# Turning node rows for the matrix multiplications: by VectorE squares and DMAs in place of TensorE transposes

## What is computed

```python
h = relu(layernorm(x));  x = x + layer1(layer0(h))
h = relu(layernorm(x));  x = x + layer2(h)
# a layer, for one graph:
u = h @ h.T / sqrt(384);  delta = softmax(u) * adjacency
attn = delta / (sum(delta, -1) + 1e-10)
ctx = upper(attn) @ (h @ wl.T + bl) + diag(attn) * (h @ ws.T + bs) + lower(attn) @ (h @ wr.T + br)
out = relu((ctx - mean(ctx)) / sqrt(var(ctx) + 1e-12) * g + beta)
```

## Time and profile before

| | |
|---|---|
| median of 3 runs | 1308.77 us (1308.66 to 1308.91) |
| profiled execution | 1309.04 us, of which the profile's span is 1307.3 us |
| TensorE (PE) busy | 1293.1 us, 99% |
| VectorE (DVE) busy | 978.3 us, 75% |
| ScalarE (ACT) busy | 854.4 us, 65% |
| GpSimd (POOL) busy | 339.5 us, 26% |
| mean granted TensorE clock | 0.994 of full speed |
| DMA engines busy | 12.9% of 16 engines, 41 GB/s |

### The profile page before, as it was taken

One profiled execution on the slowest core, in us unless ns is written; L12 is line 12 of the kernel. 1 busy time (PEld: TensorE's weight loads), 2 busy tenths in 40 slices (PEclk: granted clock), 3 DMA queues, 4 the chain that ended last, 5 costly groups with the idle time before them and its releaser, 6 DMA issues.

```text
span 1307.3 us, 28090 instructions
## 1 busy us (share of the span) xinstructions
PE 1293.1 (99%) x7820; PEld 1262.4 (97%) x7820; DVE 978.3 (75%) x3057; ACT 854.4 (65%) x2141; POOL 339.5 (26%) x438
## 2 busy tenths in 40 slices
PE   7999999999999999999999999999999999999997
PEld 5999999999999999999999999999999999999997
DVE  5777777777777677777777777778787878788776
ACT  5766666666667666666666666676666666666664
POOL 1323222222223321211111111243232332323231
PEclk8999999999999999999999999999999999999999
DMA  4101010101011110101001010130101010101111
GB/s 144 55 29 42 28 42 28 42 28 42 28 48 60 43 29 29 42 28 42 28 28 42 28 39 31 47 97 17 43 28 42 28 42 28 41 29 36 34 34 47
DMA packets 44932, 52.98 MB, mean 41 GB/s; under 512 B 3552, under 2 KB 44128, under 8 KB 44896
## 3 DMA queue, kind: packets, MB, share of 16 engines
q1 hardware_dynamic: 44896, 52.54, 12.9%
HBM read 39.94 MB, written 12.58 MB: 40 GB/s over the span
## 4 chain that ended last, share of the span: by engine, by line
PE 97%; issue 1%; DMA 1%; DVE 0%; ACT 0%; SPq 0%; POOL 0%; POOLq 0%; DVEq 0%
PE right_bank L395 23%; PE left_bank L395 23%; PE context_bank L395 23%; PE context_bank L438 16%; PE score_bank L367 5%; PE node_bank L355 5%; PE score_bank L375 1%; PE edge_bank L387 1%; DMA rows<-x 1%; ACT weight L562 0%; DVE context L744 0%; DVE in_stats L632 0%; POOL rstd L858 0%; DVE node_t L647 0%; POOLq L130 0%
## 5 line engine op out<-in xcount | busy, mean ns | idle before, releaser
L395 PE MATMUL right_bank<-weight,node_t 128*128 128x384 f32 x1728 | 368.4, 353 | 0.9 <-ACT source L491 0.9
L395 PE MATMUL left_bank<-weight,node_t 128*128 128x384 f32 x1728 | 366.6, 352 | 0.0
L395 PE MATMUL context_bank<-weight,node_t 128*128 128x384 f32 x1728 | 346.0, 343 | 0.0
L395 PEld LDWEIGHTS left_bank<-weight,node_t 128*128 128x128 f32 x1728 | 297.8, 189 | 10.6
L395 PEld LDWEIGHTS context_bank<-weight,node_t 128*128 128x128 f32 x1728 | 301.2, 188 | 3.1
L395 PEld LDWEIGHTS right_bank<-weight,node_t 128*128 128x128 f32 x1728 | 293.1, 189 | 11.2 <-issue 1.0
L438 PE MATMUL context_bank<-side_parts,attn_t 128*128 128x386 f32 x1152 | 241.1, 345 | 0.9 <-issue 0.8
L647 DVE SCALAR_TENSOR_TENSOR node_t<-node_bank,node_t 128x384 fp32r<-128x384 f32 x192 | 106.9, 557 | 155.8 <-ACT node_t L496 152.7
L438 PEld LDWEIGHTS context_bank<-side_parts,attn_t 128*128 128x128 f32 x1152 | 201.2, 190 | 1.4 <-issue 1.4
L858 POOL TENSOR_TENSOR rstd<-spread,scalars 128x2 f32<-128x2 f32 x96 | 90.2, 939 | 320.0 <-DVE spread L727 320.0
L550 ACT ACTIVATE context_bank<-context_bank,diag 128x386 f32<-128x386 f32 x192 | 105.1, 547 | 98.4 <-PE context_bank L395 98.4
(11 more groups left out here) (64 smaller groups left out, 1565.9 us busy)
## 6 DMA issues: line engine op xcount, KB each, us to landing
rows<-x SPq DMA_DIRECT2D x32, 384.0 KB, 3.2
residual_x<-x SPq DMA_DIRECT2D x32, 384.0 KB, 3.2
out<-rows SPq DMA_DIRECT2D x31, 384.0 KB, 2.6
adj_in<-adj SPq DMA_DIRECT2D x96, 64.0 KB, 2.1
piece<-weights SPq DMA_DIRECT2D x18, 192.0 KB, 2.6
rows<-weights SPq DMA_DIRECT2D x3, 576.0 KB, 9.3
vector_rows<-vectors SPq DMA_DIRECT2D x3, 576.0 KB, 5.7
vector_rows<-vectors SPq DMA_DIRECT2D x3, 384.0 KB, 6.1
```

The costliest lines, as they stand in the source:

```text
L395: mm = nc.tensor.matmul(bank[:, 0:D], node_t[:, s.parity, k, c, a], weight[:, s.phase % 2, w, c, b], start=False, stop=(c, a) == (CH - 1, ...
```

## The change

The transposes of `source` on TensorE and their two PSUM banks go. `source` becomes a view of a buffer `nodes`. ScalarE's `fill_source` now applies the relu too. VectorE's new `turn_nodes` turns all of it in one instruction, each 32 x 32 square within itself, into `turned`. SyncE's new `move_nodes` waits for that and then issues 16 DMAs, one for each pair of a source and a destination quarter of the partitions, each of 32 partitions by 192 numbers (24 KB), SBUF to SBUF, which put the squares in their places in `nodes` (the view `moved`). When all 16 have landed, ScalarE copies both tiles to `node_t` (high part) in one instruction, and VectorE makes the low part of both in one. `nodes` is single: the rows of a step are filled in only after those of the step before have been split.

The two free PSUM banks make `side_bank` double (one for each k), so `seed_side` waits for the tile before the last. Three orders change: ScalarE's body (both `fill_source` stand together behind `copy_cross`), VectorE's body (`input_shift` stands ahead of the left `split_side`, `turn_nodes(after)` behind the scores) and SyncE's (x is loaded one step earlier, and `move_nodes(after)` stands ahead of the store). The residual of phase 1 is loaded into `rows` in place of a buffer of its own. GpSimd's order stays. In the diff below the places where only names or counts follow suit are left out.

```diff
@@ -54,6 +54,9 @@
...
 PIECES = 3 * CH
+Q = 32
+QUARTERS = P // Q
+RUN = 2 * CH * Q
@@ -177,13 +180,15 @@
         first_raw = rows[:, TILES - PIECES:TILES]
-        side_bank = [bank("left_bank"), bank("right_bank")]
+        side_bank = [[bank("left_bank0"), bank("left_bank1")], [bank("right_bank0"), bank("right_bank1")]]
         context_bank = [bank("context_bank0"), bank("context_bank1")]
-        node_bank = [bank("node_bank0"), bank("node_bank1")]
...
         scores4 = score_bank[:, :].rearrange("p (k a j) -> p k a j", k=2, a=2)
-        node_3 = [b[:, 0:D].rearrange("p (c r) -> p c r", c=CH) for b in node_bank]
+        source = nodes[:, :].rearrange("p (k d) -> p k d", k=2)
+        source_blocks = nodes[:, :].rearrange("p (n q y) -> p q n y", q=QUARTERS, y=Q)
+        moved = nodes[:, :].rearrange("p (a e) -> p a e", a=QUARTERS)
+        moved_rows = nodes[:, :].rearrange("p (a n r) -> p n a r", a=QUARTERS, r=Q)
@@ -250,6 +256,10 @@
             return vector_rows[:, phase % 2, v * D:(v + 1) * D + extra]
+        def node_rows(s, part):
+            return node_t[:, s.parity, :, :, part].rearrange("p k c (a r) -> p (k c) a r", r=Q)
@@ -268,8 +278,9 @@
             def load_residual(s):
-                at_least(sp, post_done, s.tile(0))
-                sp.dma_start(residual_x[:, :, :], x_pairs[bass.ds(s.g, 1)].rearrange("g p k d -> p (g k) d")).then_inc(residual_in, 16)
+                at_least(sp, post_done, s.tile(0) - 2)
+                sp.dma_start(rows[:, bass.ds(2 * s.g, 2), :],
+                             x_pairs[bass.ds(s.g, 1)].rearrange("g p k d -> p (g k) d")).then_inc(residual_in[s.parity], 16)
@@ -302,10 +313,17 @@
...
                   .then_inc(out_written[s.parity], 16)
+            def move_nodes(s):
+                sp.wait_ge(nodes_turned, s.n + 1)
+                for a in range(QUARTERS):
+                    for q in range(QUARTERS):
+                        sp.dma_start(moved[q * Q:(q + 1) * Q, a], turned[a * Q:(a + 1) * Q, q]).then_inc(nodes_in, 16)
             def body(s):
-                prev, nxt, after = s.ahead(-1), s.ahead(1), s.ahead(2)
-                if after.exists() and after.phase == 0:
-                    load_x(after)
+                prev, nxt, after, third = s.ahead(-1), s.ahead(1), s.ahead(2), s.ahead(3)
+                if third.exists() and third.phase == 0:
+                    load_x(third)
@@ -315,6 +333,8 @@
...
                     load_norm_rows(s.phase + 1)
+                if after.exists():
+                    move_nodes(after)
@@ -328,11 +348,14 @@
...
             load_x(Step(0, 0, 1))
+            move_nodes(Step(0, 0, 0))
...
             load_first(SELF)
+            load_x(Step(0, 1, 0))
             load_norm_rows(0)
+            move_nodes(Step(0, 0, 1))
@@ -345,21 +368,10 @@
...
         def _(pe):
-            def nodes_ready(s, k):
-                pe.wait_ge(source_ready, s.tile(k) + 1)
-                at_least(pe, node_lo, s.tile(k) - 1)
-            def transpose_nodes(s, k, c):
-                mm = nc.tensor.transpose(node_bank[k][:, c * P:(c + 1) * P], source[:, k, c * P:(c + 1) * P], ident)
-                if c == CH - 1:
-                    mm.then_inc(node_moved, 1)
             def scores(s):
-                pe.wait_ge(node_hi, s.tile(2))
-                pe.wait_ge(node_lo, s.tile(2))
+                pe.wait_ge(node_hi, s.n + 1)
+                pe.wait_ge(node_lo, s.n + 1)
@@ -409,14 +419,12 @@
...
                         pe.wait_ge(piece_lo, (s.phase - 1) * PIECES + (w + 1) * CH)
-            def project_side(s, k, side, turned=None):
-                pe.wait_ge(node_hi, s.tile(k) + 1)
-                pe.wait_ge(node_lo, s.tile(k) + 1)
+            def project_side(s, k, side):
+                pe.wait_ge(node_hi, s.n + 1)
+                pe.wait_ge(node_lo, s.n + 1)
...
                 weights_split(s, k, side)
-                if turned is not None:
-                    nodes_ready(*turned)
-                project(s, k, side, side_bank[side], side_product[side], turned=turned)
+                project(s, k, side, side_bank[side][k], side_product[side])
@@ -483,17 +487,17 @@
...
             def fill_source(s, k):
-                at_least(act, node_moved, s.tile(k) - 1)
+                at_least(act, node_lo, s.n)
                 if s.phase == 1:
-                    nc.scalar.activation(source[:, k:k + 1], rows[:, s.slot(k)], ACT.Copy).then_inc(source_ready, 1)
+                    nc.scalar.activation(source[:, k:k + 1], rows[:, s.slot(k)], ACT.Relu).then_inc(source_ready, 1)
...
                     act.wait_ge(in_shift_done, s.normal + 1)
-                    nc.scalar.activation(source[:, k:k + 1], rows[:, s.slot(k)], ACT.Identity, bias=in_shift[:, k:k + 1],
+                    nc.scalar.activation(source[:, k:k + 1], rows[:, s.slot(k)], ACT.Relu, bias=in_shift[:, k:k + 1],
                                          scale=in_rstd[:, k:k + 1]).then_inc(source_ready, 1)
-            def split_nodes(s, k):
-                act.wait_ge(node_moved, s.tile(k) + 1)
-                nc.scalar.activation(node_t[:, s.parity, k, :, HI], node_3[k], ACT.Relu).then_inc(node_hi, 1)
+            def split_nodes(s):
+                act.wait_ge(nodes_in, 16 * QUARTERS * QUARTERS * (s.n + 1))
+                nc.scalar.activation(node_rows(s, HI), moved_rows, ACT.Copy).then_inc(node_hi, 1)
@@ -528,14 +532,14 @@
...
                 bias_rows_here(s, k)
-                at_least(act, side_lo[side], s.tile(k))
-                nc.scalar.activation(side_bank[side][:, 0:D], vector_row(s.phase, ROW_LEFT + side), ACT.Copy)\
+                at_least(act, side_lo[side], s.tile(k) - 1)
+                nc.scalar.activation(side_bank[side][k][:, 0:D], vector_row(s.phase, ROW_LEFT + side), ACT.Copy)\
...
                 at_least(act, context_product, s.tile(k))
-                nc.scalar.activation(side_parts[:, side, HI, 0:D], side_bank[side][:, 0:D], ACT.Copy).then_inc(side_hi[side], 1)
+                nc.scalar.activation(side_parts[:, side, HI, 0:D], side_bank[side][k][:, 0:D], ACT.Copy).then_inc(side_hi[side], 1)
@@ -565,26 +569,25 @@
...
                 if nxt.exists():
-                    split_nodes(nxt, 0)
+                    split_nodes(nxt)
...
                 seed_side(s, 1, RIGHT)
-                if nxt.exists():
-                    split_nodes(nxt, 1)
+                if len(pieces) > 0:
+                    split_piece(*pieces[0])
                 split_side(s, 0, LEFT)
+                seed_side(s, 1, LEFT)
...
                     split_edges(s)
-                seed_side(s, 1, LEFT)
...
                     copy_cross(nxt)
-                if len(pieces) > 0:
-                    split_piece(*pieces[0])
-                seed_self(s, 1)
...
                     fill_source(after, 0)
+                    fill_source(after, 1)
                 split_side(s, 1, RIGHT)
+                seed_self(s, 1)
@@ -592,12 +595,10 @@
...
                 if nxt.exists():
+                    seed_side(nxt, 0, LEFT)
+                scale_self(s, 1)
+                if nxt.exists():
                     seed_self(nxt, 0)
-                scale_self(s, 1)
-                if nxt.exists():
-                    seed_side(nxt, 0, LEFT)
-                if after.exists():
-                    fill_source(after, 1)
@@ -642,11 +642,15 @@
...
                                                ALU.mult, ALU.mult).then_inc(in_shift_done, 1)
-            def split_nodes(s, k):
-                dve.wait_ge(node_hi, s.tile(k) + 1)
-                nc.vector.scalar_tensor_tensor(node_t[:, s.parity, k, :, LO], node_3[k], 0.0,
-                                               node_t[:, s.parity, k, :, HI].bitcast(F32),
-                                               ALU.max, ALU.subtract).then_inc(node_lo, 1)
+            def turn_nodes(s):
+                dve.wait_ge(source_ready, s.tile(2))
+                at_least(dve, nodes_in, 16 * QUARTERS * QUARTERS * s.n)
+                nc.vector.transpose(turned[:, :, :], source_blocks).then_inc(nodes_turned, 1)
+            def split_nodes(s):
+                dve.wait_ge(node_hi, s.n + 1)
+                nc.vector.tensor_tensor(node_rows(s, LO), moved_rows, node_rows(s, HI).bitcast(F32), ALU.subtract).then_inc(node_lo, 1)
@@ -749,17 +753,20 @@
...
                 if s.phase == 1:
-                    dve.wait_ge(residual_in, 16 * (s.n + 1 - PAIRS))
-                other = residual_x[:, k:k + 1] if s.phase == 1 else rows[:, s.slot(k)]
-                nc.vector.scalar_tensor_tensor(rows[:, s.slot(k)], context[:, k:k + 1], 0.0, other, ALU.max, ALU.add).then_inc(post_done, 1)
+                    dve.wait_ge(residual_in[s.parity], 16 * (s.half + 1 - PAIRS // 2))
+                nc.vector.scalar_tensor_tensor(rows[:, s.slot(k)], context[:, k:k + 1], 0.0, rows[:, s.slot(k)], ALU.max, ALU.add).then_inc(post_done, 1)
...
                     input_stats(after, 0)
-                if nxt.exists():
```

(55 more changed lines are left out.)

26 lines of the change are left out of this document (10 added, 16 removed).

## The result

The changed kernel takes 1997.68 us (median of 4 runs, 1995.89 to 1997.97) against 1308.78 us before in the same runs: ratio 1.526, 95% interval 1.523 to 1.529. The direction was forecast; the size was not. 1747 us were predicted, and 1998 lies above the range.

The account below looks back on a forecast made before the run. A ring through five engines was to bound each step: engine work plus 8.65 us of DMAs, 18.0, 17.0 and 18.5 us in phases 0, 1, 2. Thirty-two of each are 1712 us, with start and tail 1747; range 1580 to 1850.

Parts of the forecast that it names:

- the term of the 16 DMAs: SP's queue, each step: fifteen distances of 0.43 us, 6.45 us; with beginning and landing 8.65 us.
- The landing: End of the moves: 2.1 us from a DMA's issue to its landing, taken from the 64 KB load.
- ring without DMAs: The engines' part of a step, from landing to first DMA issue: 9.3, 8.4 and 9.8 us by phase.
- the turn: VectorE's `turn_nodes`, 768 elements: 0.95 us, at the rate of element-wise operations, bounds 0.56 and 1.9.
- The ring: Five-engine loop from one landing of the 16 DMAs to the next; a step cannot be shorter: 18.0, 17.0, 18.5 us.
- the copies: After the landing, 768 elements each: ScalarE's copy to `node_t` 0.90 us, VectorE's `split_nodes` about 0.95 us.
- VectorE's wait for `in_rstd`: Ahead of `input_shift`, VectorE waits about 1.6 us for GpSimd in phases 0 and 2, not in phase 1.
- The clock: TensorE, idling 3 to 5 us a step, may run at half clock: costs little, or up to 96 us.
- TensorE's path: Scores, right projection and `turn_cross` end some 6 us behind the landing, against 7.8 for VectorE's path to `sum_scores`.
- Hidden moves: Rival: the ring stays hidden; faster below 0.13 us a distance, 1255 us where TensorE bounds; 7%.
- Cheap issues: Rival: SP's distances at the floor of 0.33 us, 1603 us; 15% for 1580 to 1650.
- Dear moves: Rival, with low clock: distances at 0.51 add 115 us, landing of 3.2 adds 106, slow turn 91; 16% for over 1840.

Follow-up runs that it names:

- e3: Changed kernel with its 16 moves replaced by 16 DMAs, four each of four forms (three within SBUF, one from device memory): 1932.0 us.
- e4: Changed kernel with its 16 moves replaced by eight DMAs of 128 partitions x 384 bytes, four within SBUF, four from device memory: 1464.4 us.
- e1: Changed kernel with 8 of the 16 moves of a step left out (destination quarters 2 and 3): 1481.2 us.
- e7: Changed kernel with the last 6 of 16 moves a step issued from ScalarE's queue, the first 10 from SyncE's: 1622.2 us.
- e8: Changed kernel with `nodes` double, rows filled, turned and moved three steps ahead, GpSimd and VectorE reordered, one weight piece buffer, all moves kept: 1337.6 us, ratio 1.021.
- e5: Changed kernel with GpSimd making the input's rstd ahead of the output's: 1944.3 us.
- e6: Changed kernel with 36 matmuls of unused result added on TensorE ahead of the scores, to keep it busy: 1970.8 us.
- e2: Changed kernel with 15 of the 16 moves of a step left out: 1276.4 us, ratio 0.976 against the kernel before.
- e11: Changed kernel with 12 DMAs replacing the 16 moves: four within SBUF, four SBUF to device memory, four device memory to SBUF: 1621.8 us.

## Why the prediction was wrong

**What failed: the term of the 16 DMAs.** "These are smaller (24 KB), so I take 0.43, with ends at 0.33 and 0.51." They stand 0.628 us apart, outside both ends and over the 0.5 us that the prediction itself named as a sign of being wrong: 15 x 0.198 x 96 = 285 us too little. Two things were wrong in that step. I took the highest of the three mixed distances of the earlier trace rows, 0.51, as a ceiling, where even plain loads in a row stand 0.50 apart in e3 and e4; and I let the size count in the small ones' favour, which e3 and e4 exclude. The SBUF to SBUF part, 0.1 on top, no row of before could show; the range should have been open upwards there. The landing went the other way, 1.8 us for 2.1, 29 us too much.

By phase, a step is the distance from the first of its 16 issues to the first of the next 16 (phase 0 from 310.03 to 330.04, phase 1 from 1018.19 to 1038.57 and 1059.02, phase 2 from 1515.56 to 1536.41):

```profile
1018.19 10.02 SPq L321 DMA_DIRECT2D nodes<-turned  x16
...
1038.57 10.01 SPq L321 DMA_DIRECT2D nodes<-turned  x16
...
1059.02 10.02 SPq L321 DMA_DIRECT2D nodes<-turned  x16
```

| step, us | predicted | measured |
|---|---|---|
| phase 0 | 18.0 | 20.0 |
| phase 1 | 17.0 | 20.4 |
| phase 2 | 18.5 | 20.85 |
| ring without DMAs, phase 0 | 9.3 | 8.7 |
| ring without DMAs, phase 1 | 8.4 | 9.1 |
| ring without DMAs, phase 2 | 9.8 | 9.6 |
| the turn (part of the ring), and 16 DMAs' issue and landing | 0.95 + 8.65 | 0.98 + 11.3 |

Thirty-two times the three differences are about 250 us, all that was missed. The engines' part of the ring came out right in the sum partly by luck: 0.6 and 0.2 us too much in phases 0 and 2, 0.7 too little in phase 1.

**What held.** The ring as the bound (e1, e7 and e8 shortened or opened it in three ways, and 516, 375 and, with e5's 53 in it, 660 us went), its parts on the engines within 0.7 us, the turn at 0.95 (0.98), the copies at 0.90 and 0.95 (0.84 and 0.96), VectorE's wait for `in_rstd` at 1.6 (1.51), TensorE busy 73% where 70 were said, and who waits for whom. ScalarE's wait for the moves was 7.8 us a step where some 5 were said, and not the longest of all: VectorE's behind it has 765.3 us in all, ScalarE's 751.4.

**What was only half right.** The clock: priced at nothing, or up to 96 us; it cost 27 (e6). It fell as it had behind the idle 4.04 us of the earlier trace rows: the score products, behind 4.6 and 5.0 us of idling, ran at clock 0.50, which is 1.2 GHz, in phase 0 and in phase 1 (windows: length, PE busy, clock, DMA).

```profile
303.30:304.70 1.40, 1.37 (x6) 0.50 0.01 3
...
990.64:992.00 1.36, 1.36 (x6) 0.50 0.15 55
```

The Trainium skill, page TensorE: Matmul & The Clock Gate, section HAM oscillation, describes this pattern, in which the wait of each round makes the next one start slow; the trace agrees, at 0.50 in both of these steps.

The price came up in phase 1 alone, where no wait for GpSimd covers TensorE's path to the scores. In the timeline of the changed kernel, phase 1, the right projection takes 3.08 us, where it takes 1.75 at full clock, and VectorE then waits:

```profile
992.08 3.08 PE L407 MATMUL right_bank<-weight,node_t 128*128 128x384 f32 x9
...
995.52 0.61 DVE L659 TENSOR_TENSOR score<-score_bank,cross 64x128 f32<-64x128 f32 x2 [0.76 <-PE score_bank L387]
```

The prediction let TensorE's path end some 6 us behind the landing and did not look at it again for phase 1. There VectorE was ready for the scores 6.2 us behind the landing (988.56 to 994.76, which is 995.52 less the wait of 0.76), and TensorE was not. That made phase 1, which I called the shortest step, longer than phase 0; at full clock, in e6, it is the shortest.

**The rivals.** Hidden moves did not come: 0.628 us is nearly five times the 0.13 at which it would begin. The Trainium skill, page DMA: Bandwidth & Descriptors, section Anatomy of one DMA, has about 50 ns of dispatch for GpSimd's path; on SP's queue no issue of the moves took less than 507 ns, so that figure does not carry over. Cheap issues did not come either: a move that stands alone, in e2, still holds the queue for 0.51 us.

```profile
305.18 0.51 SPq L319 DMA_DIRECT2D nodes<-turned  x1
```

And e2 shows that hidden moves were priced too low as well, 1276 us in place of 1255, since VectorE's new order costs TensorE 0.5 us a step in phase 2. "Dear moves" was the case that happened, at 16%; its bound of 0.51 kept the range too short.

## What to carry to other kernels

Count DMAs, not bytes, when one dependence waits for many of them: here each cost its issuing queue 0.5 us, 0.6 within SBUF, from 4 KB to 48 KB alike, and the next one behind them stands in the same line. Follow a new buffer once around all engines before judging it by busy times: a single buffer had made a ring of 9 + 11 us that no engine's 73% showed, and a second buffer of 3 KB a partition, with the rows filled a step earlier and a few orders changed, took 660 us off with every move kept. A bound read from a few mixed rows should stay open on the side where the new case has a feature that none of them has.

## What the runs showed of the hardware

- DMAs within SBUF issued in a row stand 0.60 to 0.63 us apart (16, 32 or 128 partitions, 128 to 768 bytes each: after, e3, e4); one alone takes 0.51 (e2). Loads from device memory stand 0.45 to 0.50 apart and stores 0.50 (32 partitions of 768 bytes, loads also 128 of 384: e3, e4, e11).
- Two queues issue side by side: SP's distance stays at 0.62 us, ScalarE's is 0.67 (e7; ScalarE's queue was not run alone).
- A VectorE transpose of 128 x 768 float32 in 32 x 32 squares took 978 ns, as long as an element-wise operation of that size (958 ns). The Trainium skill, page Vector Engine (DVE) Microarchitecture Reference, section 3.8 The reshape front-end and per-opcode configuration, has it sustain one element a cycle and lane; that it is no slower than the element-wise operation fits.
